# Mixture of experts on one Trainium2 core: where the second expert's down weights are split, and when the first row gathers are sent

## What is computed

```python
xf = x.reshape(n_tok, h)                   # 8192 rows of 256
Sm = softmax(xf @ Wr + br)                 # 8 experts
G_t, idx_t = top_k(Sm.T, 1024)             # each expert takes its 1024 best rows
tokens = xf[idx]
group = arange(8) // 2                     # two experts share one up projection
mid = silu(einsum('keh,ehf->kef', tokens, W_up[group]) + b_up[group])   # 682 wide
out = einsum('kef,efh->keh', mid, W_down) + b_down
y = zeros_like(xf).at[idx].add(G[..., None] * out)
```

## Time and profile before

| | us |
|---|---|
| median of 3 runs | 2457.08 (2451.19 to 2457.49) |
| the profiled execution's own time | 2457.34 |
| its span in the profile | 2455.3 |
| PE busy in the span | 2240.3 (91%) |
| DVE, ACT, POOL busy | 1461.8, 861.8, 374.3 |
| the changed stage in the span | about 580 to 892 |

### The profile page before, as it was taken

One profiled execution on the slowest core, in us unless ns is written; L12 is line 12 of the kernel. 1 busy time (PEld: TensorE's weight loads), 2 busy tenths in 40 slices (PEclk: granted clock), 3 DMA queues, 4 the chain that ended last, 5 costly groups with the idle time before them and its releaser, 6 DMA issues. The chain is left out here.

```text
span 2455.3 us, 40334 instructions
## 1 busy us (share of the span) xinstructions
PE 2240.3 (91%) x15302; PEld 1932.5 (79%) x15303; DVE 1461.8 (60%) x3147; ACT 861.8 (35%) x1210; POOL 374.3 (15%) x352
## 2 busy tenths in 40 slices
PE   7999998536999958999998699999999999999998
PEld 4888887325988856787787588888888888888887
DVE  6787876583445436777776584554544545545544
ACT  2455554122454413454443432222222222222222
POOL 3111110204557540111110410000000000000000
PEclk9999999755999979999999799999999999999999
DMA  2121211203435331111111400000000000000000
GB/s 73 53 68 60 77 60 47 61 0 102 74 71 105 57 52 35 52 68 60 60 52 52 144 28 27 27 3 25 26 26 26 26 26 26 26 26 26 26 9 9
DMA packets 110137, 115.05 MB, mean 47 GB/s; under 512 B 16080, under 2 KB 98768, under 8 KB 110032
## 3 DMA queue, kind: packets, MB, share of 16 engines
q1 hardware_dynamic: 97744, 96.49, 12.4%
q0 software_dynamic: 12288, 17.05, 4.2%
HBM read 62.92 MB, written 50.59 MB: 46 GB/s over the span
## 5 line engine op out<-in xcount | busy, mean ns | idle before, releaser
L1857 DVE TENSOR_TENSOR zmix_hid<-zmix_act_gate,psum 128x1024 f32<-128x1024 f32 x128 | 156.3, 1221 | 372.0 <-issue 346.7
L143 PE MATMUL psum<-zmix_wd_hi,zmix_hid_hi 128*128 128x256 f32 x1024 | 289.5, 283 | 2.3 <-DVE zmix_acc L1848 2.3
L145 PE MATMUL psum<-zmix_wd_hi,zmix_hid_lo 128*128 128x256 f32 x1024 | 289.8, 283 | 0.0
L144 PE MATMUL psum<-zmix_wd_lo,zmix_hid_hi 128*128 128x256 f32 x1024 | 289.7, 283 | 0.0
L1808 ACT ACTIVATE zmix_hid_hi<-zmix_hid 128x1024 fp32r<-128x1024 f32 x128 | 135.5, 1059 | 395.2 <-PE psum L145 276.7
L1800 ACT ACTIVATE zmix_act_gate<-psum 128x1024 f32<-128x1024 f32 x128 | 131.6, 1028 | 378.0 <-PE psum L145 378.0
L604 PE MATMUL psum<-att_v_cur,att_probs 128*128 128x96 f32 x2048 | 252.7, 278 | 4.5 <-ACT att_probs L732 3.1
L604 PEld LDWEIGHTS psum<-att_v_cur,att_probs 128*128 128x128 f32 x2048 | 240.8, 193 | 14.5 <-ACT att_probs L732 4.0
L1862 DVE TENSOR_TENSOR zmix_hid_lo<-zmix_hid,zmix_hid_hi 128x1024 fp32r<-128x1024 f32 x128 | 157.8, 1232 | 135.2 <-ACT zmix_hid_hi L1808 134.3
L1848 DVE SCALAR_TENSOR_TENSOR zmix_acc<-psum,zmix_weight,zmix_acc 128x256 f32<-128x256 f32 x512 | 211.7, 475 | 1.6 <-PE psum L145 1.6
L143 PE MATMUL psum<-zmix_xT_hi,zmix_wg_hi 128*128 128x512 f32 x512 | 201.9, 394 | 11.2 <-DVE zmix_xT_lo L1837 11.2
(11 more groups left out here) (288 smaller groups left out, 4534.1 us busy)
## 6 DMA issues: line engine op xcount, KB each, us to landing
x<-att_x_new SPq DMA_DIRECT2D x32, 512.0 KB, 2.9
att_x_in<-in_x SPq DMA_DIRECT2D x16, 512.0 KB, 3.8
rows<-att_normed_new SPq DMA_DIRECT2D x16, 512.0 KB, 3.0
att_x_in<-x SPq DMA_DIRECT2D x16, 512.0 KB, 3.9
turned<-att_newT SPq DMA_DIRECT2D x16, 512.0 KB, 2.8
zmix_xn<-turned SPq DMA_DIRECT2D x16, 512.0 KB, 4.4
zmix_acc<-x SPq DMA_DIRECT2D x16, 512.0 KB, 4.2
out_x<-zmix_acc SPq DMA_DIRECT2D x16, 512.0 KB, 3.2
```

The lines of the kernel that those rows point to most:

```text
L143: pe.matmul(out, st_hi, mv_hi, start=first, stop=False)
L144: pe.matmul(out, st_hi, mv_lo, start=False, stop=False)
L145: return pe.matmul(out, st_lo, mv_hi, start=False, stop=last)
L1857: dve.tensor_tensor(hid[:, :, :], act_gate[:, :, :], psum[:, 2:4, :], ALU.mult).then_inc(up_out, 1)
```

## The change

The split of the second expert's down weights leaves the end of a group. It now stands inside the group that uses it, behind the first block: on ACT behind `hidden` of block 0, on DVE behind `hidden_lo` of block 0. The end of a group splits the first expert's down weights alone. Ahead of the loop, the split of expert 1's down weights goes (the loop does it), and expert 0's low part stands behind the first `rows_lo`. POOL sends the eight gathers of expert 0 ahead of the six memsets. PE's wait for the memsets moves from the head of the stage to `down` of block 0.

```diff
@@ gpsimd @@
+            for h in range(2):
+                gather(0, 0, h)
             for p in range(2):
                 pool.memset(mid_lo[BIAS_ROW:, p, FC - 1, :].bitcast(F32), 0.0).then_inc(cleared, 1)
                 pool.memset(mid_hi[BIAS_ROW:, p, FC - 1, :].bitcast(F32), 0.0).then_inc(cleared, 1)
...
             pool.wait_ge(cleared, 6)
-            for h in range(2):
-                gather(0, 0, h)
             iterations(pool, body)
@@ tensor, down(g, j) @@
+                if j == 0:
+                    pe.wait_ge(cleared, 6)
                 pe.wait_ge(lo_made, done(PAIRS + 1, g, PAIRS + 1))
...
-            pe.wait_ge(cleared, 6)
             turn(0, 0, 0)
@@ scalar, body(q, last) @@
                     hidden(q * GJ + j, j % 2, q * EP + j // 2)
+                    if j == 0:
+                        act.wait_ge(down_made[1], q * (EP * HT))
+                        down_weights(q * EP + 1, 1)
                 if not last:
                     up_weights(q + 1)
-                    for i in range(EP):
-
-                        act.wait_ge(down_made[1], q * (EP * HT) + (i + 1) * HT)
-                        down_weights(q * EP + EP + i, i)
+                    act.wait_ge(down_made[1], q * (EP * HT) + HT)
+                    down_weights(q * EP + EP, 0)

             up_weights(0)
             down_weights(0, 0)
-            down_weights(1, 1)
             iterations(act, body)
@@ vector, body(q, last) @@
+                    if j == 0:
+                        down_weights(q * EP + 1, 1)
                     if j >= 1:
                         out(j - 1)
...
                 out(GJ - 1)
-                if not last:
-                    down_weights(q * EP + EP + 1, 1)

             up_weights(0)
+            rows_lo(0, 0, 0, 0)
             down_weights(0, 0)
-            rows_lo(0, 0, 0, 0)
-            down_weights(1, 1)
             iterations(dve, body)
```

## The result

| | before | changed |
|---|---|---|
| median of 8 runs | 2453.36 (2450.01 to 2457.49) | 2444.48 (2440.63 to 2446.55) |
| ratio, 95% interval | 1 | 0.9960 (0.9949 to 0.9970) |
| profiled execution, its span | 2457.34, 2455.3 | 2440.63, 2438.6 |
| PE busy | 2240.3 | 2230.6 (91%) |
| DVE, ACT, POOL busy | 1461.8, 861.8, 374.3 | 1460.7, 862.4, 373.3 |

The change saves 0.4%, about 9 us (the interval gives 7.4 to 12.5). The time lies at the lower edge of the range, inside it; what I had held likeliest, no change that can be told, was wrong. The forecast of 2452.0 missed by 7.5 us. Half of that is the kernel before: its median was 2457.08 over 3 runs and is 2453.36 over 8. The other half is the gain, 8.9 instead of 5.1.

What follows compares the result with a forecast made beforehand. PE, busy 91%, was taken as the bound, losing time in this stage only at the head and three boundaries; 3.5 (head) + 3.2 (boundaries) - 1.6 (clock) = 5.1 us, so 2452.0 us, range 2444 to 2458.

Steps and rivals of the forecast that it cites:

- no change that can be told: Whole kernel: a change too small to measure, within about 0.3% (7.4 us); chance 0.64.
- The boundaries together: Three group boundaries: the `xT_lo` wait goes, a gather wait follows; gains 1.7, 0.3 and 1.2, together 3.2 us.
- POOL's quickening: Boundaries: POOL's copy and gathers run quicker without `wd_lo` beside them; nothing at the first, 0.1 second, 1.2 third.
- I expect the same fate in as many boundaries as before: Boundaries: new waits about as long as the old, so PE's clock falls at two of three; costs 1.6 us.
- rival 2: Boundaries: gathers bind but the clock holds; 3.5 + 3.2 + 1.4 = 8.1 us, so 2449.0; chance 0.25.
- I take 3.5: up 0 at 593.6: Stage's head: gathers sent ahead of memsets let up 0 begin 3.5 us earlier, bounds 2.2 to 4.3.
- The contention term: Stage's head: two more 135 KB gathers among weight loads on the DMA engines, at 348 GB/s, cost 0.8 us.
- Rival 1: Boundaries: freed whole, gathered rows in time after all; 15.7 us gained, so 2441.4; chance 0.08.
- Rival 3: Stage's head: gives nothing, early gathers only share loaded DMA engines; 1.6 us gained, so 2455.5; chance 0.10.
- Rival 4: Boundaries: the moved `wd_lo` lands on the gathers and delays rows; 3.1 us slower, 2460.2; chance 0.07.

Runs made afterwards that it cites:

- the split alone: Changed kernel with POOL's head order undone (memsets before gathers), moved split kept: 2448.48 against 2455.30 for the kernel before, ratio 0.9972.
- the later load: Changed kernel with SP waiting for the first gathered rows before its first down-weight load: 2444.99 against 2454.70 for the kernel before, ratio 0.9969.
- the head alone: Kernel before with gathers ahead of memsets, their wait in down 0, `rows_lo` ahead of down weights; second expert's split unmoved: 2456.15 against 2455.30, ratio 1.001.
- The later gathers: Changed kernel with a spare-tile memset on POOL ahead of each group's first gathers: 2454.34 against 2454.70 for the kernel before, ratio 0.9997.

## Why the prediction was wrong

Right were the order of events and most causes. ACT is free when up 0 begins, `xT_lo` is in time, the gathers are late next, one chunk pair on, and the moved split costs PE nothing. The fourth gather at the head was issued as early as reckoned (4.3). The sizes failed, all three in the sum of 5.1, where the stage won 11.1:

- **"The boundaries together: 1.7 + 0.3 + 1.2 = 3.2 us"** measured 2.35 + 1.5 + 2.2 = 6.1. The step that failed is POOL's quickening, taken as nothing at the first boundary, 0.1 at the second and "a half" at the third. From POOL's copy to the fourth gather's issue end it took 7.42, 8.10 and 9.09 before, and 6.85, 6.91 and 6.83 with the change: 0.6, 1.2 and 2.3 won. Issue to use was 1.90, 1.80 and 1.89 instead of 1.97. So the waits were 1.7, below my 2.4 to 2.8. The gain lies in gathers that I had not read. These rows of the kernel before show a held gather at each boundary, and the second boundary's copy:

```profile
677.44 1.64 POOL L1298 DMA_INDIRECT moe_rows<-rows,moe_idx_get  x1 [0.30 <-issue]
...
747.62 1.61 POOL L1291 COPY moe_idx_get<-lists_idx 128x8 int32 x1
...
751.57 1.66 POOL L1298 DMA_INDIRECT moe_rows<-rows,moe_idx_get  x1 [0.30 <-issue]
...
822.75 1.80 POOL L1298 DMA_INDIRECT moe_rows<-rows,moe_idx_get  x1 [0.90 <-POOL moe_idx_get L1291]
```

With the change the four gathers of each boundary take 0.94 to 1.04. At the third that returned 0.8 (of the 1.80) and 1.0 (of the 1.93 that I had read), at the first and second 0.7 each. The copy returned about a third of its excess, not a half: it still takes 1.06, 1.10 and 1.11, which is 0.5 less than before at the second and third and 0.1 more at the first. It ended 0.04 or 0.05 behind DVE's subtraction at every boundary, before (820.22 + 1.63 = 821.85 against 821.81) and after (666.68 against 666.63), so its share could have been worked out from where the `mid_lo` piece would end. The Trainium skill (SBUF — State Buffer, SBUF: two separate sides) calls the port pair that DVE and GpSimd share an exclusive lock for the whole instruction, for a DVE operation with two SBUF inputs against a GpSimd one that reads SBUF. For these six copies the trace agrees.
- **"I expect the same fate in as many boundaries as before", -1.6**: the clock fell at none. The reason given was that the new waits are as long as the old, and that rested on the term above. Over all profiles, no single wait of 1.62 to 1.75 at a boundary was followed by a fall in the twelve boundaries of the change, its repeat, the split alone and the later load; behind waits of 2.37 to 2.51 it fell four times and held three times; behind 3.08 to 3.21 it fell three times of three. Of two waits close together, the kernel before had one fall behind 1.70 and 1.98; its second profile held behind 1.28 and 2.04, and the head alone behind 1.97 and 1.88. The later gathers show that the length of the wait matters: put the waits at 3.1 and the falls come back, with everything else as in the change. The term should have been +1.6, the old loss at the third (I had read 1.4, from its first chunk alone). That was rival 2, which I gave 0.25; its sum of 8.1 carried the 3.2 and was short by that.
- **The head, "I take 3.5: up 0 at 593.6"**, is 2.55 up to up 0, and 3.1 with the half clock behind it, inside the bounds of 2.2 to 4.3. The contention term, 0.8 for two more gathers at the rate of the window, was 3.67 - 1.97 = 1.7: it left out the load of the down matrix beside them. The later load shows it, with 1.85 from issue to use. The other 0.6 I had not counted: up 0 ran less of its time at half clock.
- **The parts as a sum.** I added head and boundaries as if each stood alone. The head alone gives nothing and with the split 3.2. The split alone gives 7.9, so this error of method didn't hurt the forecast, but it would have ruined one for either part.

Together: 5.1 + 2.9 (boundaries) + 3.2 (clock, from -1.6 to +1.6) + 0.3 (the down block) - 0.4 (head, 3.1 for 3.5) = 11.1. Rival 1 was wrong, the rows do bind. Rival 3 was wrong here; for the head alone its number came true by luck, since up 0 did begin early there and the loss came from ACT. Rival 4 was wrong, since `wd_lo` began 12.7 behind up 0 as reckoned, and the fourth gather had gone out at 10.95.

The chances followed from the same step: with waits put at 1.7, shorter than the 2.42 behind which the clock had fallen and the 2.51 behind which it had held, more weight belonged to rival 2.

## What to carry to other kernels

When a wait is removed, read the whole queue of the engine that is late next, at every boundary and not only at one, and lay each of its instructions beside what the other engines will then run: here that was 3 us. A wait on TensorE is priced by its length and by what it does to the clock, so shortening a wait of 2.4 us to 1.7 was worth more than 0.7 in this stage. And test parts of a change together as well as alone: an early start pays only if nothing behind it was counting on the old order.

## What the runs showed of the hardware that I had not expected

- A gather's issue that begins inside one of DVE's subtractions of two SBUF tiles is held. Of 247 that began 0.04 or more after such a subtraction, with 0.25 or more of it left, in the stage of all twelve profiles, every one ended 0.80 to 0.92 behind the subtraction and took 1.10 to 2.51 (674.22 + 1.64 = 675.86 behind 673.28 + 1.76 = 675.04). The 30 that began within 0.03 of the subtraction's start took 0.94 to 1.02 (669.02 beside 669.01). Alone a gather takes 0.94 to 1.04, the very first of the stage 1.18. So a held gather can be worked out from where DVE's subtraction ends. Why those that begin together go free is open.
- The six copies of the index list above ended with the subtraction. One did so although it had begun first: in the second profile of the kernel before one began at 742.69, the subtraction at 742.91, and the copy took 2.01. Four others, which began 0.03 to 0.17 ahead, kept their 0.2; what parts them is open.
- A fall of the clock in this stage costs 1.4 to 1.6 us. Whether it comes behind 2.4 us of idling is not the kernel's to say: the same kernel fell at its first and third boundary once, and at its first and second the other time.
- A gather's issue to use took 1.8 to 2.0 us at five places, and 3.67 beside the load of a 768 KB down matrix.
